# Three rows in flight for V, four for the experts, and a first tile started in another order

## The chip, the cores and the metric

The kernel runs on one core of a Trainium2 chip. The number that counts is the device time of one execution in microseconds, as the median over runs; less is better. The engines of the core are called by the profile's names: PE (TensorE), DVE (VectorE), ACT (ScalarE), POOL (GpSimd) and SP (SyncE, which only issues transfers here). PSUM is divided into eight banks, numbered 0 to 7.

## What is computed

A graph of N = 1250 nodes with 768 features runs through two graph attention layers and then through one transformer block. Cut to what matters:

```python
def _gat_layer(x, W, a_src, a_dst, b, src, dst, n):
    h = x @ W
    e = leaky_relu((h @ a_src)[src] + (h @ a_dst)[dst], 0.2)
    w = exp(e - segment_max(e, dst)[dst])
    alpha = w / segment_sum(w, dst)[dst]
    return segment_sum(h[src] * alpha[:, None], dst) + b

x = x + gat2(relu(gat1(layernorm(x))))          # 1250 x 768
x = x + ffn(layernorm(x))
def ffn(x):
    x = x + attention(layernorm(x) * g1 + b1)   # 12 heads of 64, x @ Wqkv, softmax, @ Wproj
    return x + moe(layernorm(x) * g2 + b2)      # 8 experts, top 2, 768 -> 384 -> 768, exact gelu
```

## The kernel before

Everything is float32 in quality: each product is made of three matmuls of rounded parts (`three`, lines 368 to 370: high by high, low by high, high by low). For each operand ACT copies the high part out of PSUM or SBUF ("hi", "higher"), and DVE or POOL subtracts it from the original to get the low part ("lo", "lower"). The 1250 nodes are ten tiles of 125 rows (T = 10). The order on each engine is written out by hand; semaphores are counted, and a wait such as `wait_ge(sem("tile_lo"), ...)` holds back everything behind it on its engine. Three stages matter here.

**The second graph layer.** For each tile t, ACT and DVE make a row block of attention weights in `lg2[:, t % 2]` (`sloped`, `leaky` L687, `exponential`, `weigh` L693). PE transposes it into banks 0 to 2 (`turned`, L591), ACT and DVE split the result into `pthi` and `ptlo` (`higher` L641, `lower` L698), and PE sums over the neighbours with 60 matmuls (`sums`, L368 to L370). `turned` of tile t+1 waits for `lower` of tile t, since both use banks 0 to 2. `agg_pe` gives PE's order: it turns tile t+1 ahead of the sums of tile t. `agg_act` and `agg_dve` give the others', with a step k for each tile. In steps 3 to 12 of this layer, `finish2` adds the sums to the residual, DVE takes mean and variance, ACT the root (`root`), DVE the reciprocal, and ACT writes two normalized rows (`rows2` L1847: `xab` and `xnb`). SP sends them to DRAM as `xa_d` and `xn_d` (`g2_rows`, L1356).

**The V stage.** V is the product of the normalized rows with a third of Wqkv. SP loads a tile of `xn_d` back into one of two buffers `vtin` (`v_in`, L1365). DVE applies scale and offset (`v_affine`, L565 and L567, 125x768 each). PE transposes into banks 0 and 1 (`v_turn`, L522, 6 instructions). ACT and DVE split (`v_higher` L543, `v_lower` L554). PE multiplies in two halves of 18 matmuls (`v_half`). The PE order is turn, half, turn, half: turn i+1 is followed by half i % 2 of tile i // 2, and the other halves come later, beside the first query-key work, which starts with `project`. `v_turn` of tile t waits for `v_lower` of tile t-1 (one pair of banks), and `v_in` of tile t for `v_turn` of tile t-2 (two buffers). `v_affine(3)` and later ones stand on DVE directly ahead of the `v_lower` of the tile before.

**The experts.** The (token, expert) pairs are sorted into TILES = 27 tiles of 128 slots. For tile j, POOL gathers 128 rows of 776 floats by an index (`gather`, L1557) into buffer j % 3. PE transposes them (`turn`, L1229), multiplies with W1 (`hidden`), transposes the gelu (`turn_h`, L1247) and multiplies with W2 (`output`). ACT and DVE split W1 and W2 anew for each tile (`split_w1`: L1892, L2382; `split_w2`: L1900, L2389, each 128x2304). ACT writes the weighted result (`row`, L1927), and POOL adds its rows to the output in DRAM by two indirect transfers, one for first and one for second choices (`add_first` L1563, `add_second` L1571). W2 comes through SP (L1437) into one of two buffers, issued when the `w2lo` of two tiles before is done. PE's order in the loop is hidden(i+1), turn(i+2), output(i), turn_h(i+1). POOL's is

```python
gather(0); gather(1); gather(2); gather(3)
pool.wait_ge(sem("route_dve"), ADDS)
for j in range(TILES):
    if j + 4 < TILES:
        gather(j + 4)
    add_first(j)
    add_second(j)
```

where `gather(j)` from j = 3 on waits until tile j-3 is transposed and its `weight` (L2408) is taken, and `add_first(j)` waits for `row(j)`.

## Time and profile before

| what | value |
|---|---|
| median of three runs | 1574.52 us (1572.43 to 1579.07) |
| the profiled execution: its own time, its span | 1568.86 us, 1567.1 us |
| PE, DVE, ACT, POOL busy | 91%, 74%, 62%, 32% of the span |
| mean granted TensorE clock | 0.964 of full speed |
| second layer from its first turn | about 419 to 543 us of the span |
| V stage (to the start of `project`) | about 543 to 592 us |
| experts | about 1334 to 1563 us |

Times below are microseconds from the start of the span, except durations in ns where the view says so. A row of the timeline is: start, duration, engine, line, operation, output tile <- input tiles, shapes, and in brackets how long the engine was idle before it and what it had waited for. PEclk is the granted clock as a share of full speed (2.4 GHz); 0.5 is 1.2 GHz. A matmul's duration overlaps the next one's, so starts are compared, not sums of durations.

### The profile page before, as it was taken

The page shows a single profiled execution, that of the slowest core. Times are in us where ns is not written, and L with a number is a line of the kernel's source. Part 1 is how long each engine was busy: PE and PEld are TensorE (multiplying, and loading weights), DVE is VectorE, ACT ScalarE, POOL GpSimd, SP SyncE. Part 2 cuts the span into 40 slices and gives each one's busy share as a digit, 9 for nine tenths or more (in the row PEclk, how much of TensorE's full clock was granted, in tenths as well). Part 3 has the DMA queues.
Part 4 walks back from the last instruction along what each step waited for, and adds up shares of the span by engine and source line. Part 5 has one row for each costly group of instructions (what it writes and reads, how often), then busy time and mean ns, then how long its engine had stood idle before and what let it go on. Part 6 is the DMA issues. An engine that isn't in the chain of part 4 may idle for free.

```text
span 1567.1 us, 25494 instructions
## 1 busy us (share of the span) xinstructions
PE 1424.7 (91%) x8979; PEld 1343.9 (86%) x8979; DVE 1154.7 (74%) x1752; ACT 968.8 (62%) x1656; POOL 508.2 (32%) x365
## 2 busy tenths in 40 slices
PE   3998799999699979999999999999988996799996
PEld 1896488999699979899898998989988996799995
DVE  6788889625779652486868868688687887788884
ACT  7996976522568322366857667576777311788884
POOL 2000000000000001244636446364466310488886
PEclk9999699999799999999999999999999997899998
DMA  7001000221225440000000000000001594699883
GB/s 196 2 1 41 1 10 21 82 85 53 100 64 162 137 149 1 1 21 1 21 0 0 20 0 20 0 0 0 20 22 41 163 282 94 213 251 249 244 231 102
DMA packets 59910, 121.49 MB, mean 78 GB/s; under 512 B 11152, under 2 KB 27156, under 8 KB 59824
## 3 DMA queue, kind: packets, MB, share of 16 engines
q1 hardware_dynamic: 48448, 98.09, 20.0%
q0 software_dynamic: 11376, 22.29, 6.6%
q8 instruction: 49, 0.80, 0.2%
q14 instruction: 37, 0.30, 0.1%
HBM read 89.57 MB, written 44.31 MB: 85 GB/s over the span
## 4 chain that ended last, share of the span: by engine, by line
PE 59%; DVE 10%; DMA 6%; issue 4%; ACT 2%; POOL 2%; ACTq 0%; SPq 0%; POOLq 0%; DVEq 0%
PE ps L368 11%; PE ps L369 11%; PE ps L370 11%; DMA xg<-xg_d,index 4%; PE ps L808 4%; PE ps L849 4%; PE ps L851 3%; PE ps L828 3%; PE ps L850 3%; PE ps L830 3%; DVE mcol L1050 2%; DMA vtin<-xn_d 2%; PE ps L591 1%; DVE prlo L1019 1%; PE ps L817 1%
## 5 line engine op out<-in xcount | busy, mean ns | idle before, releaser
L1019 POOL TENSOR_TENSOR prlo<-prob,prhi 125x500 fp32r<-125x500 f32 x180 | 249.0, 1389 | 273.0 <-ACT prob L961 272.3
L1050 DVE TENSOR_REDUCE mcol<-ps 125x1 f32<-125x1250 f32 x120 | 175.0, 1458 | 78.2 <-PE ps L808 77.6
L959 ACT ACTIVATE prhi<-ps 125x500 fp32r<-125x500 f32 x300 | 177.0, 590 | 74.9 <-PE ps L830 69.4
L849 PE MATMUL ps<-prhi,vhi 125*128 125x250 f32 x600 | 173.1, 288 | 10.4 <-POOL prlo L1019 4.8
L961 ACT ACTIVATE prob<-ps 125x500 f32<-125x500 f32 x300 | 176.4, 588 | 2.1 <-DVE prlo L1019 2.0
L1506 POOL MEMSET q<- 128x2500 f32 x1 | 2.2, 2187 | 532.4 <-PE ps L370 532.4
L851 PE MATMUL ps<-prlo,vhi 125*128 125x250 f32 x600 | 169.2, 282 | 0.0
L850 PE MATMUL ps<-prhi,vlo 125*64 125x250 f32 x600 | 168.2, 280 | 0.0
L1648 PE MATMUL ps<-ohs,ohd 128*125 128x417 bf16 x380 | 124.2, 389 | 39.2 <-DVE ohs L2063 38.6
L828 PE MATMUL ps<-qst,kst 128*125 128x250 f32 x600 | 156.6, 284 | 3.4 <-issue 1.4
L830 PE MATMUL ps<-q,k 128*125 128x250 f32 x600 | 153.7, 280 | 0.0
L368 PE MATMUL ps<-hhi,pthi 125*125 125x384 f32 x400 | 150.3, 376 | 0.0
L1019 DVE TENSOR_TENSOR prlo<-prob,prhi 125x500 fp32r<-125x500 f32 x120 | 106.9, 892 | 48.4 <-ACT prob L961 47.4
L369 PE MATMUL ps<-hhi,ptlo 125*125 125x384 f32 x400 | 136.2, 341 | 0.0
L370 PE MATMUL ps<-hlo,pthi 125*125 125x384 f32 x400 | 135.5, 339 | 0.0
L849 PEld LDWEIGHTS ps<-prhi,vhi 125*128 125x128 f32 x600 | 114.8, 191 | 16.9 <-DVE prlo L1019 6.6
L2063 DVE TENSOR_SCALAR ohs<-iota,scol,sval 128x420 bf16<-128x420 f16 x380 | 123.5, 384 | 0.0
L828 PEld LDWEIGHTS ps<-qst,kst 128*125 128x125 f32 x600 | 113.0, 188 | 10.6 <-issue 3.8
L1774 ACT ACTIVATE ohd<-iota,drel 128x125 bf16<-128x125 f16 x380 | 118.8, 389 | 0.3 <-POOLq L1473 0.3
L851 PEld LDWEIGHTS ps<-prlo,vhi 125*128 125x128 f32 x600 | 114.6, 191 | 0.0
L830 PEld LDWEIGHTS ps<-q,k 128*125 128x125 f32 x600 | 113.3, 189 | 0.0
L1648 PEld LDWEIGHTS ps<-ohs,ohd 128*125 128x125 bf16 x380 | 55.0, 146 | 66.8 <-DVE ohs L2063 46.7
(324 smaller groups left out, 4057.8 us busy)
## 6 DMA issues: line engine op xcount, KB each, us to landing
w2st<-in_L_ffn_W_dram SPq DMA_DIRECT2D x27, 1152.0 KB
w1all<-in_L_ffn_W_dram SPq DMA_DIRECT2D x8, 1152.0 KB, 9.3
wqst<-in_L_ffn_Wqkv_dram SPq DMA_DIRECT2D x12, 384.0 KB, 4.3
hid_d<-tin SPq DMA_DIRECT2D x10, 375.0 KB
hin<-hid_d SPq DMA_DIRECT2D x10, 375.0 KB
vtin<-xn_d SPq DMA_DIRECT2D x10, 375.0 KB
out_dram<-accr POOLq DMA_DIRECT2D x10, 375.0 KB, 9.0
xall<-in_x_dram SPq DMA_DIRECT2D x5, 672.0 KB
```

Source lines behind the costliest of these rows:

```text
L368: pe.matmul(o, lhi, rhi, start=start, stop=False)
L369: pe.matmul(o, llo, rhi, start=False, stop=False)
L370: return pe.matmul(o, lhi, rlo, start=False, stop=stop)
L828: pe.matmul(o, kst[:, e, kt * P:(kt + 1) * P], qst[:, e, g * GQ:(g + 1) * GQ], start=True, stop=False)
L830: last = pe.matmul(o, k2[:, e, kt * P:(kt + 1) * P], q2[:, e, g * GQ:(g + 1) * GQ], start=False, stop=True)
L849: pe.matmul(ps[:, b:b + GQ], vhi[:, e, kt, :], hi, start=kt == 0, stop=False)
L850: pe.matmul(ps[0:HD, b:b + GQ], vlo[:, e, kt, :], hi, start=False, stop=False)
L851: last = pe.matmul(ps[:, b:b + GQ], vhi[:, e, kt, :], lo, start=False, stop=kt == T - 1)
L959: act.activation(prhi[:, n % RING, :], bank(3 + n % 3, P, 2 * GQ), ACT.Exp, scale=float(HD) ** -0.5)
L1019: eng.tensor_tensor(prlo[:, n % RING, :], prob[:, n % 3, :], prhi[:, n % RING, :].bitcast(f32), ALU.subtract)\
L1050: dve.tensor_reduce(mcol[:, e, t:t + 1], ps[0:P, 0:N], AX.X, ALU.max, negate=True).then_inc(sem("max"), 1)
L1648: pe.matmul(into, hots(b)[:, i, :], ohs[:, g % OHS, 0:PACK], start=u == 0, stop=u == WINDOW - 1).then_inc(sem("oh_free"), 1)
```

## The change

Three parts.

1. V stage. `vtin` has three buffers. `v_turn` uses banks 0 and 1 for even tiles and 2 and 3 for odd ones, and so waits for `v_lower` of tile t-2. `v_in(0)`, `v_in(1)` and `v_in(2)` are issued on SP after `g2_rows(3)`, `(4)` and `(5)`, `v_in(3)` after `g2_rows(8)`, and `v_in(4)` now after `g2_rows(9)`. From tile 3 on, `v_in` waits for `v_turn` of tile t-3. On DVE the affine steps of tiles 0 to 2 move to steps 7 to 9 of the second layer, and later ones stand two tiles ahead and behind `v_lower`. On ACT `v_higher(2)` moves ahead of the root of tile 9.
2. Second layer, tile 0. PE makes the first half of tile 0's sums ahead of the turn of tile 1; ACT makes `higher(0)` ahead of `exponential(1)`, DVE `weigh(0)` ahead of `leaky(1)` and `lower(0)` ahead of `weigh(1)`.
3. Experts. A fourth buffer `xg3` (in the place of a tile that is dead by then); `gather(j)` waits for tile j-4, and one more gather stands ahead of the first add.

```diff
-    vtin = put("vtin", [P, 2, D], f32, at=put.end)
+    vtin = put("vtin", [P, 3, D], f32, at=put.end)
...
+    xg3 = put("xg3", [S, ROW], f32, at=put.end - 4 * D)
...
         def rows(j):
-            return xg2[:, :] if j % 3 == 2 else xg[:, j % 3, :]
+            return (xg[:, 0, :], xg[:, 1, :], xg2[:, :], xg3[:, :])[j % 4]
...
         def v_turn(pe, t):
-            u = t % 2
-            if t == 0:
+            if t < 2:
                 pe.wait_ge(sem("agg_lo"), 2 * T + 1)
             else:
-                pe.wait_ge(sem("tile_lo"), 2 * T + t + 2)
+                pe.wait_ge(sem("tile_lo"), 2 * T + t + 1)
             pe.wait_ge(sem("v_row"), t + 1)
             for k in range(KD):
-                at = k // 3 * BANK + k % 3 * P
-                last = pe.transpose(ps[:, at:at + P], vtin[:, u, k * 128:(k + 1) * 128], ident[0:P, 0:P])
+                at = (t % 2 * 2 + k // 3) * BANK + k % 3 * P
+                last = pe.transpose(ps[:, at:at + P], vtin[:, t % 3, k * 128:(k + 1) * 128], ident[0:P, 0:P])
...
             turned(pe, n, 0, 0)
+            sums(0, 0, range(T))
+            turned(pe, n, 1, 1)
+            sums(0, 0, range(T, 2 * T))
             with pe.Fori(0, T // 2 - 1) as i:
-                turned(pe, n, 2 * i + 1, 1)
-                sums(2 * i, 0)
                 turned(pe, n, 2 * i + 2, 0)
                 sums(2 * i + 1, 1)
-            turned(pe, n, T - 1, 1)
-            sums(T - 2, 0)
+                turned(pe, n, 2 * i + 3, 1)
+                sums(2 * i + 2, 0)
             v_turn(pe, 0)
             sums(T - 1, 1)
...
             maximum(1)
+            weigh(dve, n, 0)
             leaky(dve, n, 1)
-            weigh(dve, n, 0)
             maximum(2)
...
             for t in range(T - 2):
                 g2_rows(t)
-                if t == 3:
-                    v_in(0)
-                    v_in(1)
-            v_in(2)
+                if 3 <= t < 6:
+                    v_in(t - 3)
             g2_rows(T - 2)
             v_in(3)
+            g2_rows(T - 1)
             v_in(4)
-            g2_rows(T - 1)
             v_in(5)
...
             def gather(j):
-                if j >= 3:
-                    pool.wait_ge(sem("rows_raw"), T + j - 2)
-                    pool.wait_ge(sem("gslot"), j - 2)
+                if j >= 4:
+                    pool.wait_ge(sem("rows_raw"), T + j - 3)
+                    pool.wait_ge(sem("gslot"), j - 3)
...
             pool.wait_ge(sem("route_dve"), ADDS)
+            gather(4)
             for j in range(TILES):
-                if j + 4 < TILES:
-                    gather(j + 4)
+                if j + 5 < TILES:
+                    gather(j + 5)
                 add_first(j)
                 add_second(j)
...
                 if k == T + 1:
                     v_higher(act, 1)
+                    v_higher(act, 2)
...
-                if k in (T - 2, T - 1):
-                    v_affine(dve, k - (T - 2))
-                if k == T:
-                    v_lower(dve, 0)
-                    v_affine(dve, 2)
-                if k == T + 1:
-                    v_lower(dve, 1)
+                if T - 3 <= k < T:
+                    v_affine(dve, k - (T - 3))
+                if k in (T, T + 1):
+                    v_lower(dve, k - T)
             agg_dve(dve, order, 1, before2, finish2, after2)
+            v_affine(dve, 3)
             for t in range(2, T):
-                if t + 1 < T:
-                    v_affine(dve, t + 1)
                 v_lower(dve, t)
+                if t + 2 < T:
+                    v_affine(dve, t + 2)
```

DVE at the start of the second layer, before (L673 to L682 are the maximum of a tile, L687 `leaky`, L693 `weigh`):

```order
L687 SCALAR_TENSOR_TENSOR lg2_66<-esb_65,ed_55,lg2_66 125x1250 [waits agg_sl]
L693 SCALAR_TENSOR_TENSOR lg2_66,wsum_58<-lg2_66,cnt_63 125x1250 [waits agg_e]
L673 ISA cand_67,zsum_57<-esb_65,far_64 125x1250 [waits far_ready]
```

And the same place of the changed kernel (L695 is `weigh`, L689 `leaky`):

```order
L695 SCALAR_TENSOR_TENSOR lg2_66,wsum_58<-lg2_66,cnt_63 125x1250 [waits agg_e]
L689 SCALAR_TENSOR_TENSOR lg2_66<-esb_65,ed_55,lg2_66 125x1250 [waits agg_sl]
L675 ISA cand_67,zsum_57<-esb_65,far_64 125x1250 [waits far_ready]
```

The weights of tile 0 are now finished one 125x1250 pass earlier.

SP's queue at the end of the second layer, before, from the load of row tile 2 to that of tile 5 (`vtin` is the tile's buffer; the rows between are the outputs of tiles 8 and 9):

```order
L1365 DMA vtin<-xn_d 125x768 [waits xn_out,tile_raw]
L1356 DMA out_dram<-xres 112x768 [waits x1_row]
L1356 DMA out_dram<-xres 13x768
L1356 DMA xa_d<-xab 112x768 [waits xa_row]
L1356 DMA xa_d<-xab 13x768
L1356 DMA xn_d<-xnb 112x768 [waits xn_row]
L1356 DMA xn_d<-xnb 13x768
L1365 DMA vtin<-xn_d 125x768 [waits xn_out,tile_raw] x2
```

And of the changed kernel, from the outputs of tile 9 on (L1361 is the line of the outputs, L1370 that of the loads):

```order
L1370 DMA vtin<-xn_d 125x768 [waits xn_out,tile_raw]
L1361 DMA out_dram<-xres 112x768 [waits x1_row]
L1361 DMA out_dram<-xres 13x768
L1361 DMA xa_d<-xab 112x768 [waits xa_row]
L1361 DMA xa_d<-xab 13x768
L1361 DMA xn_d<-xnb 112x768 [waits xn_row]
L1361 DMA xn_d<-xnb 13x768
L1370 DMA vtin<-xn_d 125x768 [waits xn_out,tile_raw] x2
```

In the first of these the pair of loads is that of tiles 3 and 4, behind the outputs of tile 8. In the second it is that of tiles 4 and 5, behind the outputs of tile 9; tile 3's is the row at the top. The load of tile 2 is gone from here to a place three output groups earlier.

POOL at the start of the experts, before:

```order
L1557 DMA xg_145<-xg_d,index_176 128x776 [waits gates_out,route_dve,sum_out1,sum_out0]
L1557 DMA xg_145<-xg_d,index_176 128x776
L1557 DMA xg2_194<-xg_d,index_176 128x776
L1557 DMA xg_145<-xg_d,index_176 128x776 [waits gslot,rows_raw]
L1557 DMA xg_145<-xg_d,index_176 128x776 [waits gslot,rows_raw,route_dve]
L1563 DMA out_0_dram<-yrow_146,index_176 1250x768 [waits y_row2]
```

And of the changed kernel:

```order
L1560 DMA xg2_195<-xg_d,index_176 128x776
L1560 DMA xg3_181<-xg_d,index_176 128x776
L1560 DMA xg_145<-xg_d,index_176 128x776 [waits gslot,rows_raw,route_dve]
L1560 DMA xg_145<-xg_d,index_176 128x776 [waits gslot,rows_raw]
L1566 DMA out_0_dram<-yrow_146,index_176 1250x768 [waits y_row2]
```

The fourth gather waits for nothing more, and a sixth stands ahead of the first add.

## Rows read from the trace of the kernel before

**Rows 1.** The page: the chain that ended last, shares of the span by line.

```profile
PE ps L368 11%; PE ps L369 11%; PE ps L370 11%; DMA xg<-xg_d,index 4%; PE ps L808 4%; PE ps L849 4%; PE ps L851 3%; PE ps L828 3%; PE ps L850 3%; PE ps L830 3%; DVE mcol L1050 2%; DMA vtin<-xn_d 2%; PE ps L591 1%; DVE prlo L1019 1%; PE ps L817 1%
```

**Rows 2.** Busy time by stretch: length, five engines, PEclk, DMA share, GB/s.

```profile
407.00:427.00 20.00, 7.33 (x30) 5.89 (x29) 18.35 (x30) 13.54 (x15) 0.00 (x0) 0.65 0.56 196
451.00:520.00 69.00, 69.00 (x415) 69.00 (x415) 59.81 (x113) 53.65 (x59) 0.00 (x0) 1.00 0.45 143
543.00:592.00 49.00, 38.30 (x216) 36.23 (x215) 27.48 (x36) 15.36 (x19) 10.30 (x5) 0.93 0.41 126
1352.00:1381.00 29.00, 29.00 (x181) 28.55 (x179) 25.75 (x25) 25.73 (x24) 18.21 (x8) 1.00 0.84 235
1381.00:1540.00 159.00, 149.98 (x901) 144.47 (x901) 131.27 (x120) 131.09 (x120) 136.95 (x61) 0.99 0.88 243
```

**Rows 3.** Waits from 1352 to 1541 us: us in total, times, longest.

```profile
PEld ps L1229 <- DMA xg<-xg_d,index: 13.9, 16, 2.3
```

**Rows 4.** Timeline of PE, experts: the turns of tiles 3, 4, 25 and 26.

```profile
1359.19 0.82 PE L1229 MATMUL ps<-ident,xg 128*128 128x128 f32 x6
...
1366.46 0.82 PE L1229 MATMUL ps<-ident,xg 128*128 128x128 f32 x6
...
1531.19 0.87 PE L1229 MATMUL ps<-ident,xg 128*128 128x128 f32 x6 [1.94 <-DMA xg<-xg_d,index]
...
1540.05 0.81 PE L1229 MATMUL ps<-ident,xg 128*128 128x128 f32 x6
```

**Rows 5.** Timeline of POOL: gathers of tiles 3, 6 and 26, first add.

```profile
1341.85 0.95 POOL L1557 DMA_INDIRECT xg<-xg_d,index  x1 [4.54 <-DVE gjunk L2408]
...
1360.65 2.58 POOL L1563 DMA_INDIRECT out_dram<-yrow,index  x1 [8.67 <-ACT yrow L1927]
...
1374.53 2.61 POOL L1557 DMA_INDIRECT xg<-xg_d,index  x1 [0.30 <-PE ps L1229]
...
1529.86 2.63 POOL L1557 DMA_INDIRECT xg<-xg_d,index  x1 [0.30 <-ACT yrow L1927]
```

**Rows 6.** Timeline of DVE, experts: a low part of W2, one of W1.

```profile
1370.24 2.56 DVE L2389 TENSOR_TENSOR w2lo<-w2st,w2hi 128x2304 fp32r<-128x2304 f32 x1 [0.28 <-ACT w2hi L1900]
...
1373.69 2.56 DVE L2382 TENSOR_TENSOR w1lo<-w1all,w1hi 128x2304 fp32r<-128x2304 f32 x1 [0.43 <-ACT w1hi L1892]
```

**Rows 7.** Timeline of ACT, experts: the high part of W2, two tiles on.

```profile
1383.10 2.14 ACT L1900 ACTIVATE w2hi<-w2st 128x2304 fp32r<-128x2304 f32 x1
```

**Rows 8.** The page: transfer issues, KB each, median us from issue to landing.

```profile
w1all<-in_L_ffn_W_dram SPq DMA_DIRECT2D x8, 1152.0 KB, 9.3
```

**Rows 9.** The chain in order of time, V stage: start, us, what.

```profile
534.60 6.79 DMA vtin<-xn_d
...
541.41 0.97 DVE vtin L565
...
545.37 1.03 ACT xab L1847
...
548.22 7.52 DMA vtin<-xn_d
```

**Rows 10.** Timeline of PE, V stage: turns of tiles 4 and 9, `project`.

```profile
564.10 0.80 PE L522 MATMUL ps<-ident,vtin 125*128 125x125 f32 x6
...
588.41 0.86 PE L522 MATMUL ps<-ident,vtin 125*128 125x125 f32 x6 [1.94 <-DVE xtlo L554]
...
592.26 0.35 PE L368 MATMUL ps<-xthi,wqhi 128*128 128x418 f32 x1
```

**Rows 11.** Timeline of PE, second layer: turns 0, 1, first sum, turn 2.

```profile
418.88 2.46 PE L591 MATMUL ps<-ident,lg 125*125 125x125 f32 x10 [9.33 <-DVE lg L693]
...
424.35 2.43 PE L591 MATMUL ps<-ident,lg 125*125 125x125 f32 x10 [3.01 <-DVE ptlo L699]
...
426.44 0.66 PE L368 MATMUL ps<-hhi,pthi 125*125 125x384 f32 x1
...
438.64 1.25 PE L591 MATMUL ps<-ident,lg 125*125 125x125 f32 x10
```

More of the change, by code:

```diff
@@ L543, in v_higher @@
             act.activation(xthi[:, :, t * P:(t + 1) * P].rearrange("p (a k) c -> p a k c", a=2),
-                           two(0, 128, 3 * P).rearrange("p a (k c) -> p a k c", k=3), ACT.Copy).then_inc(sem("tile_hi"), 1)
+                           two(t % 2 * 2, 128, 3 * P).rearrange("p a (k c) -> p a k c", k=3), ACT.Copy).then_inc(sem("tile_hi"), 1)
         def v_out(act, t):
@@ L606, in agg_pe, with sums @@
         def agg_pe(pe, n):
-            def sums(t, u):
-                for i in range(2 * T):
+            def sums(t, u, steps=range(2 * T)):
+                for i in steps:
                     triple_sum(pe, n, t, u, i)
             turned(pe, n, 0, 0)
+            sums(0, 0, range(T))
+            turned(pe, n, 1, 1)
+            sums(0, 0, range(T, 2 * T))
             with pe.Fori(0, T // 2 - 1) as i:
-                turned(pe, n, 2 * i + 1, 1)
-                sums(2 * i, 0)
                 turned(pe, n, 2 * i + 2, 0)
                 sums(2 * i + 1, 1)
-            turned(pe, n, T - 1, 1)
-            sums(T - 2, 0)
+                turned(pe, n, 2 * i + 3, 1)
+                sums(2 * i + 2, 0)
             v_turn(pe, 0)
@@ L658, in agg_act @@
             for k in range(T + 3):
+                if k == 0:
+                    higher(act, n, 0)
                 if k + 1 < T:
@@ L715, in step @@
             def step(k):
+                if k == 0:
+                    lower(dve, n, 0)
                 if k + 1 < T:
                     weigh(dve, n, k + 1)
-                if k < T:
+                if 0 < k < T:
                     lower(dve, n, k)
@@ L995, in attention_act @@
             for t in range(T // 2 - 1):
-                v_higher(act, 2 * t + 2)
+                if t:
+                    v_higher(act, 2 * t + 2)
                 v_higher(act, 2 * t + 3)
```

20 lines of the change are left out of this document (10 added, 10 removed).

## The prediction

> **What bounds the kernel now.** I read the chain that ended last first. Most of the lines that it names are products on PE, but two entries are transfers that PE ends up waiting for: the gather of the experts' rows, 4% of the span, and the load of V's rows, 2% [rows 1]. Those are the two transfers that the change gives more buffers. I then read the busy time by stretch [rows 2]. PE is busy without a gap in the second layer from 451 to 520 us, and also at the start of the experts (29.00 of 29.00 us). It is not busy in three places: from 407 to 427 us, where the second layer starts (7.33 of 20 us, at a granted clock of 0.65); from 543 to 592 us, the V stage (38.30 of 49 us, clock 0.93); and in the experts from 1381 to 1540 us (149.98 of 159 us). The change touches exactly those three, and PE's order of work is otherwise the same, so the sum is made of what each gives back.
>
> **Experts: a fourth buffer.** No computation is added or removed. There are 27 gathers and 54 adds as before; only the order on POOL moves by one gather. At its best PE takes one tile in 1366.46 - 1359.19 = 7.27 us, from the turn of tile 3 to that of tile 4 [rows 4]. From the turn of tile 4 to that of tile 26 it needs 173.6 us for 22 tiles, 7.89 us each. At 7.27 it would be 159.9 us, so 13.7 us are lost. The list of waits puts them down to one cause: the weight load of the transpose waits for the gather 16 times, 13.9 us in all [rows 3].
>
> Why does the gather come late? The first one that waits for nothing takes POOL 0.95 us; that of tile 6 takes 2.61 us and begins while DVE is inside `w1lo` [rows 5]. DVE's pass ends at 1376.25, and the gather ends 0.89 us after it, at 1377.14 [rows 6]. So the gather has to wait for the end of the pass and then takes its usual time. POOL goes at DVE's pace, not at its own. After the descriptors are out, the rows need 4 to 6 us more (tile 25 and others), and the turn is due some 4.3 us later: there is no slack. The gather of tile j in the changed kernel stands where that of tile j-1 stood, a full tile earlier, and so gains about 7.3 us of slack against lateness of at most 2.3 us [rows 3]. What it has to wait for, the turn and the weight of tile j-4, is done long before. The extra gather falls into the 8.67 us in which POOL waits for the first result [rows 5], so it costs nothing. If that cover were gone it would cost 3 us once. Queued behind each gather are the two adds of its round, and they are served as before.
>
> Upper bound: all 13.7 us. Lower bound: POOL keeps the pace that it shows from tile 6 to tile 26, 155.3 us for 20 gathers, 7.77 us each [rows 5]; then the last gather still comes one place earlier, and PE's end, which hangs on it, moves up by 7.7 us. I take 12, near the upper one: at 7.27 us a tile the transfer share of 0.88 becomes 0.88 x 7.89 / 7.27 = 0.95, and a few waits should remain.
>
> The Trainium skill has a rule on this, "SBUF — State Buffer", section "Who interferes with whom": a DVE instruction with two SBUF inputs and a GpSimd instruction that reads SBUF shut each other out for a whole instruction. By that rule, the trace agrees: 2.61 us against 0.95 us. The rule speaks against the change in one way: if the lockout makes POOL the slowest engine, more buffers move the gathers only once, and the experts give 7.7 us and not 12.
>
> **V stage.** Nothing is computed more or less here either. Before, the chain runs: DVE stands still until the load of tile 2, issued at 534.60, has landed after 6.79 us; the affine passes follow at 541.41; only then come DVE's statistics for tile 8, ACT's normalized rows at 545.37, SP's outputs and, behind them, the next load at 548.22, which takes 7.52 us [rows 9]. With the change tile 2 is loaded three output groups earlier, so its affine steps are done in the second layer, where DVE is busy 59.8 of 69 us and PE covers it [rows 2]. Then PE goes on from 543 us with turn 1, a half, turn 2 and another half without waiting: turn plus half is 592.26 - 588.41 = 3.85 us [rows 10]. Turn 3 starts at about 551.
>
> The next thing to be late is the load of tile 4. It now stands on SP behind the outputs of tile 9, and those stand behind ACT's `v_higher(2)`. My reckoning, in the clock of the trace before: turn 2 done 547.5, `v_higher(2)` 0.8, the root and DVE's reciprocal 0.7, two rows of ACT 1.9 (1.03 each at most [rows 9]), SP's outputs 0.9: issue at 551.8. The load takes 6.8 to 7.5 us [rows 9], and two affine passes of 0.97 us follow [rows 9]: turn 4 at 560.7 to 561.3, say 561.0. Before it is at 564.10 [rows 10], so 3.1 us are won up to here. PE waits some 5.5 us for it and runs at half clock after that. What half clock costs I take from the second layer: PE's first sums take 438.64 - 426.44 = 12.2 us [rows 11], where at full clock 70 instructions take 70 x 69 / 415 = 11.6 us [rows 2], less 1.1 for the turn, 10.5: an extra 1.7 us. From turn 4 to `project` there are six turns and halves, 6 x 3.85 = 23.1 us, plus 1.7: 24.8 us, and `project` starts at 585.8. Later loads are issued when the turn of three tiles before is done, 11.5 us ahead of need against 6 to 7.5 us of load, and hide. Before, `project` starts at 592.26. V gives 6.5 us. Bounds: if the loads of tiles 6 to 9 stay chained, only 3; if the load of tile 4 took no wait at all, 592.26 less (543 + 9 x 3.85) = 14.6. I stay with 6.5, since SP's order leaves the load of tile 4 where it is.
>
> **Second layer, tile 0.** DVE's `weigh(0)` is one pass of 1.4 us earlier, so turn 0 starts at 417.5 and ends at 419.9. The split takes the 3.0 us that it takes now (421.34 to 424.35) [rows 11]. The sums start at 422.9 and not at 426.44. They and turn 1 take 10.5 + 1.1 us at full clock, and half clock adds 1.7 us, or 2.7 us if it lasts as long after the restart as it does now. Turn 2 then starts at 436.2 to 437.2 and not at 438.64: 1.4 to 2.4 us, I take 1.9. Nothing is behind it: turn 2 needs `weigh(2)` and `lower(1)`, done some 2 us ahead. If these were late, it would be 0. From turn 2 on PE is the bound until 543 us, so the gain is carried through.
>
> **Sum.** 12.0 + 6.5 + 1.9 = 20.4 us. The profiled execution took 1568.86 us, its span being 1567.1, and would become 1548.5. The median of the three runs is 1574.52, 5.7 above it; taken from that, 1554.1 us.
>
> **Rivals.** Half a per cent is 7.9 us, about what can be told from no change here.
>
> *POOL's pace.* The lock makes POOL itself the slowest engine in the experts. For it: POOL's gaps are 0.30 us throughout [rows 5]. Against it: PE went at 7.27 us with the same adds and gathers beside it, and POOL's alone need 5 us. Experts 7.7: 1574.5 - 16.1 = 1558.4.
>
> *Transfers fill up, no gain in the experts.* W2's load is issued when `w2lo` of tile 3 ends, at 1372.80 [rows 6], and is needed by `w2hi` of tile 5 at 1383.10 [rows 7]: 10.3 us. Loads of the same size needed 9.3 us in the stage before [rows 8]. A faster pace loads the transfer engines more (share 0.95), and once the load takes over 10.3 us ACT waits. At 11.5 us a tile lasts 7.89 us again and the experts give nothing: 1574.5 - 8.4 = 1566.1. Against it: ACT never waits for W2 now, at a share of 0.84 and a pace of 7.27 us [rows 2].
>
> *The same, to a loss.* The other two parts give 8.4 us, so the experts would have to lose 16.3 us for the whole to be 7.9 us slower: 0.7 us in each of 24 tiles, 8.6 us a tile. W2's load has two tiles less 4.2 us, so it decides from 13.0 us on, 3.7 us over the row. At 8.7 us a tile the time is about 1585.
>
> *V stays chained.* ACT's and DVE's new places make tile 9's outputs later still, and with them the loads: V gives 3 and not 6.5, 1557.6. I count it with the forecast.
>
> **How the numbers follow.** Forecast, with V chained or not: 0.70. POOL's pace: 0.14. Transfers without a gain: 0.10. The loss: 0.03. Another effect of any sign: 0.03. All of the first two are faster than by 0.5%, and half of the third: 0.88 with a little of the last. Within 0.5%: 0.08; slower: 0.04. Range: the lower end is 13.7 + 2.4 + 9 = 25 us off and 3 us for the spread of medians, 1546. The upper end takes in POOL's pace, with a V stage at its lower bound and 3 us of spread, and reaches toward the third case: 1564.
>
> **What the profile would show.** Right: turns of tiles 5 to 26 every 7.3 to 7.4 us with hardly any wait for the gather, and gathers of 2.6 us as before; the second layer's turn 2 some 12 us after the first sums; turn 4 of V after a wait of about 5 us, for the load, and none after that. Wrong: ACT's `w2hi` waiting for its load; POOL's gathers 7.7 us apart and PE waiting for them; a `project` later than 43 us after the second layer's last sum; turn 2 of the second layer waiting for `weigh(2)`.

## The result and the profile after

The changed kernel takes 1558.61 us, the median of 4 runs (1551.40 to 1560.81); the kernel before took 1573.47 beside it (4 runs). The ratio is 0.9893, with a 95% interval of 0.985 to 0.9936: 14.9 us by the medians, 16.8 by the ratio, where 20.4 were forecast. A second measurement of the same code on another occasion gave 1552.15 us, ratio 0.9897 (0.9867 to 0.9927). The predicted 1554 lies between the two medians, but the second was taken where the kernel before ran at 1569.70 us, 3.8 us less than beside the first. What was saved is 15 to 17 us both times, and 20.4 were forecast.

The profiled execution took 1560.81 us, the slowest of its four. Read stage by stage, it shows less in the experts than the forecast. The windows of the changed kernel (length, PE, PEld, DVE, ACT, POOL busy, PEclk, DMA share, GB/s), against [rows 2]:

```profile
541.00:587.00 46.00, 37.29 (x222) 36.20 (x222) 26.80 (x31) 13.42 (x17) 10.13 (x5) 0.93 0.38 119
1345.00:1425.00 80.00, 80.00 (x498) 79.26 (x497) 71.96 (x67) 70.00 (x65) 63.73 (x27) 1.00 0.85 240
1425.00:1530.00 105.00, 98.36 (x596) 94.36 (x594) 87.31 (x81) 88.04 (x80) 92.81 (x41) 1.00 0.85 239
```

For 80 us PE has no gap in the experts, which the kernel before managed for 29. After that it is idle again, 6.6 us in 105. The last of the three rows also points at the reason: POOL is busy 92.81 us, and its 41 instructions each stand behind a gap of 0.30 us, 12.3 us in all. Together that is 105.1, the whole window: POOL never waits for work there. Its busy time holds the time in which DVE's passes hold it up, so it is not all work of its own.

The waits from 1345 to 1532 us (us in total, times, longest), against [rows 3]:

```profile
PEld ps L1234 <- DMA xg<-xg_d,index: 10.6, 11, 1.8
...
ACT w2hi L1905 <- DMA w2st<-in_L_ffn_W_dram: 1.4, 3, 0.8
```

PE's turns in the experts, tiles 4, 12, 14 and 26, against [rows 4]:

```profile
1361.30 0.82 PE L1234 MATMUL ps<-ident,xg 128*128 128x128 f32 x6
...
1419.32 0.82 PE L1234 MATMUL ps<-ident,xg 128*128 128x128 f32 x6
...
1435.02 0.88 PE L1234 MATMUL ps<-ident,xg 128*128 128x128 f32 x6 [0.74 <-DMA xg<-xg_d,index]
...
1530.49 0.88 PE L1234 MATMUL ps<-ident,xg 128*128 128x128 f32 x6 [1.12 <-DMA xg<-xg_d,index]
```

From tile 4 to tile 12 a tile takes (1419.32 - 1361.30) / 8 = 7.25 us, as forecast. From tile 12 to tile 26 it takes 111.17 / 14 = 7.94. Over all 22 tiles 169.2 us stand against 173.6 before: 4.4 us, not 12 to 13.7, and less than the 7.7 that the forecast gives as its lower bound. What happened between is on POOL (L1560 the gather, L1566 and L1574 the two adds), gathers 9 to 13:

```profile
1383.89 2.60 POOL L1560 DMA_INDIRECT xg<-xg_d,index  x1 [0.30 <-PE ps L1234]
...
1395.91 3.01 POOL L1574 DMA_INDIRECT out_dram<-yrow,index  x1 [0.30 <-issue]
1399.22 2.09 POOL L1560 DMA_INDIRECT xg<-xg_d,index  x1 [0.30 <-issue]
1401.62 3.72 POOL L1566 DMA_INDIRECT out_dram<-yrow,index  x1 [0.30 <-DVE gjunk L2411]
1405.64 3.15 POOL L1574 DMA_INDIRECT out_dram<-yrow,index  x1 [0.30 <-ACT yrow L1932]
1409.10 3.37 POOL L1560 DMA_INDIRECT xg<-xg_d,index  x1 [0.30 <-issue]
...
1420.10 2.72 POOL L1560 DMA_INDIRECT xg<-xg_d,index  x1 [0.30 <-issue]
```

These four rounds take 36.21 us, 9.05 each. At 7.25 they would take 29.0, so POOL loses 7.2 us, one tile, while PE loses nothing yet: its next turns still come 7.24 to 7.26 us apart, on gathers that POOL had made ahead (its lead). From tile 13 on that lead is gone. The same stretch on ACT and DVE:

```profile
1392.77 2.13 ACT L1905 ACTIVATE w2hi<-w2st 128x2304 fp32r<-128x2304 f32 x1 [0.76 <-DMA w2st<-in_L_ffn_W_dram]
```

```profile
1394.94 2.56 DVE L2392 TENSOR_TENSOR w2lo<-w2st,w2hi 128x2304 fp32r<-128x2304 f32 x1 [1.14 <-ACT w2hi L1905]
...
1397.88 2.55 DVE L2385 TENSOR_TENSOR w1lo<-w1all,w1hi 128x2304 fp32r<-128x2304 f32 x1
...
1401.33 2.56 DVE L2392 TENSOR_TENSOR w2lo<-w2st,w2hi 128x2304 fp32r<-128x2304 f32 x1
```

W2's load was 0.76 us late for ACT. DVE's `w2lo` came later, `w1lo` then followed it closely, and the next `w2lo` began at 1401.33, 6.39 us after the late one, at once behind DVE's other work. POOL's first add began at 1401.62, the usual 0.30 us after the gather's end at 1401.31, and met `w2lo` 0.29 us into its pass. (The profile names `gjunk`, DVE's weight pass, as its releaser, but `add_first` waits in the code for ACT's row alone, and that was ready at 1398.18.) It ended at 1405.34, 1.45 us after the pass, and took 3.72 us instead of 1.57.

The V stage, PE's turns 1, 4 and 7 and `project`, against [rows 10]:

```profile
541.72 0.80 PE L522 MATMUL ps<-ident,vtin 125*128 125x125 f32 x6
...
560.69 1.49 PE L522 MATMUL ps<-ident,vtin 125*128 125x125 f32 x6 [7.01 <-DVE vtin L566]
...
575.50 0.83 PE L522 MATMUL ps<-ident,vtin 125*128 125x125 f32 x6 [1.49 <-DVE vtin L566]
...
586.95 0.35 PE L369 MATMUL ps<-xthi,wqhi 128*128 128x418 f32 x1
```

and the chain in order of time (start, us, what), against [rows 9]:

```profile
550.57 8.00 DMA vtin<-xn_d
...
...
562.21 8.19 DMA vtin<-xn_d
570.42 3.95 DVE vtin L564
```

From turn 1 to `project` it takes 586.95 - 541.72 = 45.23 us. Before, turn 1 began at 542.90 and `project` at 592.26, 49.36 us. V has given 4.1 us.

The second layer's first turns (turns 0 and 2 on L590, and one instruction of the stage ahead on L490), against [rows 11]:

```profile
410.09 0.48 PE L490 MATMUL ps<-diag,ones 125*125 125x125 f32 x2 [0.33 <-DVE diag L474]
418.47 2.46 PE L590 MATMUL ps<-ident,lg 125*125 125x125 f32 x10 [7.90 <-DVE lg L695]
...
437.46 1.25 PE L590 MATMUL ps<-ident,lg 125*125 125x125 f32 x10
```

From the stage ahead to turn 2 it is 27.37 us. Before, that instruction stood at 409.06 and turn 2 at 438.64, 29.58 us: 2.2 us won.

### The profile page after: what moved, and what is told of

Read it like the earlier page. It is cut to its first block, busy times and chain, and to the rows that moved or that the text cites. A ratio compares the mean times of both kernels' runs of the same rounds, so it can differ in the third digit from the quotient of the medians.

```text
span 1558.9 us, 25492 instructions
## 1 busy us (share of the span) xinstructions
PE 1420.0 (91%) x8979; PEld 1342.8 (86%) x8979; DVE 1160.3 (74%) x1752; ACT 969.1 (62%) x1656; POOL 513.1 (33%) x365
## 4 chain that ended last, share of the span: by engine, by line
PE 62%; DVE 9%; DMA 5%; issue 3%; ACT 2%; POOL 2%; POOLq 0%; DVEq 0%; ACTq 0%; SPq 0%
PE ps L369 12%; PE ps L370 12%; PE ps L371 12%; PE ps L812 4%; PE ps L853 4%; PE ps L855 3%; PE ps L832 3%; PE ps L854 3%; PE ps L834 3%; DMA xg<-xg_d,index 3%; DVE mcol L1055 2%; PE ps L590 1%; DMA vtin<-xn_d 1%; DVE prlo L1024 1%; PE ps L821 1%
## 5 line engine op out<-in xcount | busy, mean ns | idle before, releaser
L1024 DVE TENSOR_TENSOR prlo<-prob,prhi 125x500 fp32r<-125x500 f32 x120 | 112.1, 935 | 46.7 <-ACT prob L965 45.7
L853 PEld LDWEIGHTS ps<-prhi,vhi 125*128 125x128 f32 x600 | 115.2, 192 | 16.8 <-DVE prlo L1024 7.1
L832 PEld LDWEIGHTS ps<-qst,kst 128*125 128x125 f32 x600 | 112.8, 188 | 10.5 <-issue 3.8
```

The costliest lines, as they stand in the source:

```text
L832: pe.matmul(o, kst[:, e, kt * P:(kt + 1) * P], qst[:, e, g * GQ:(g + 1) * GQ], start=True, stop=False)
L853: pe.matmul(ps[:, b:b + GQ], vhi[:, e, kt, :], hi, start=kt == 0, stop=False)
L1024: eng.tensor_tensor(prlo[:, n % RING, :], prob[:, n % 3, :], prhi[:, n % RING, :].bitcast(f32), ALU.subtract)\
```

## The experiments

Below, POOL is "in step" as long as its gathers follow each other at PE's pace, 7.25 us a tile, and "out of step" where they take longer. Two theories of what limits the experts are tested: (1) POOL's instructions beside DVE's long passes, once POOL has fallen out of step; (2) the transfers. Every kernel here was timed against the kernel before on its own chip, whose median there was 1569.7 to 1571.4 us; only ratios and traces are compared across chips.

**p_experts, p_v, p_first: one part of the change each; p_all: all of it again.** The edits are the three parts of the diff, here with a line or two of each.

```diff
 p_experts
-            return xg2[:, :] if j % 3 == 2 else xg[:, j % 3, :]
+            return (xg[:, 0, :], xg[:, 1, :], xg2[:, :], xg3[:, :])[j % 4]
 p_v
-    vtin = put("vtin", [P, 2, D], f32, at=put.end)
+    vtin = put("vtin", [P, 3, D], f32, at=put.end)
 p_first
             leaky(dve, n, 0)
             maximum(1)
+            weigh(dve, n, 0)
             leaky(dve, n, 1)
-            weigh(dve, n, 0)
```

> The kernel before with the four buffers of gathered rows in the experts alone. The recorded prediction gives this part 12.0 us (7.7 to 13.7). The trace of the changed kernel shows less: from turn 4 to turn 26 of the experts 169.2 us where the kernel before took 173.6, so 4.4 us, plus about 1.7 us for the missing wait of turn 3 to 4. Theory 1 (after tile 9 POOL needs more than 7.26 us for a tile, since its gathers and adds find no gap between VectorE's passes with two operands in SBUF): turns 4 to 12 are 7.26 us apart, then the gaps grow to about 8 us, because POOL loses a tile of lead; time 5 to 8 us below the kernel before. Theory 2 (the transfers are the limit): the same time, but then the gathers of POOL wait for nothing of VectorE and TensorE waits for gathers that were issued in time. The slip seen in the changed kernel's trace may also be a matter of the moment at which this loop starts; then turns stay 7.26 us apart to the end here and the time is 11 to 13 us below the kernel before.

> The kernel before with the V stage's two pairs of banks and three row buffers alone. The recorded prediction gives this part 6.5 us (3 to 14.6). The trace of the changed kernel shows 49.4 us from the second turn to the projection before and 45.2 us after: 4.1 us, with one wait of 7.0 us at turn 4 for the load of tile 4 and one of 1.5 us at turn 7. If the parts add, the time is 4 to 5 us below the kernel before; the end of the V stage at about 587 to 588 us instead of 592.3.

> The kernel before with the second layer's first tile in the other order alone. The recorded prediction gives this part 1.9 us (1.4 to 2.4); the trace of the changed kernel shows 2.2 us against the end of the stage ahead. Expected 2 us below the kernel before; a loss would say that what was gained there is lost in the work behind it.

> The changed kernel again, on the same chip as the three parts, to see whether they add up. The recorded prediction gives 20.4 us, the first measurement gave 14.9 us. If the loss against the prediction is POOL's lost tile of lead in the experts (theory 1), then executions without that loss would be faster by up to 7 or 8 us than those with it, and the times of this kernel spread more than those of the kernel before. If the transfers are the limit (theory 2), the times lie close together at 13 to 16 us below the kernel before.

Measured, all on one chip:

| kernel | median us | lowest to highest | ratio, 95% interval | from the ratio | forecast |
|---|---|---|---|---|---|
| before | 1569.70 (23 runs) | 1566.42 to 1574.83 | | | |
| p_experts | 1558.74 (6) | 1555.29 to 1560.83 | 0.9924, 0.9908 to 0.9941 | 11.9 us | 12.0 |
| p_v | 1564.26 (12) | 1560.82 to 1571.10 | 0.9973, 0.9958 to 0.9987 | 4.2 us | 6.5 |
| p_first | 1568.73 (12) | 1561.57 to 1571.95 | 0.9991, 0.9977 to 1.0005 | 1.4 us | 1.9 |
| p_all | 1552.15 (6) | 1549.11 to 1564.98 | 0.9897, 0.9867 to 0.9927 | 16.2 us | 20.4 |

The parts add up within the intervals: 11.9 + 4.2 + 1.4 = 17.5 us against 16.2 together. `p_first` alone can't be told from no change. The experts' part, which my reading of the first trace had put at 5 to 8 us, gives all of the forecast's 12 (9.3 to 14.4 by the interval). The trace of `p_all` says why the first trace misled. In the experts, PE's turns of tiles 4 and 26:

```profile
1365.49 0.82 PE L1234 MATMUL ps<-ident,xg 128*128 128x128 f32 x6
...
1525.04 0.82 PE L1234 MATMUL ps<-ident,xg 128*128 128x128 f32 x6
```

159.55 us for 22 tiles, 7.25 each, with no wait for a gather after the first tile's. One round of POOL there, gather, two adds and the next gather, and DVE's `w2lo` in it:

```profile
1395.31 2.62 POOL L1560 DMA_INDIRECT xg<-xg_d,index  x1 [0.30 <-ACT yrow L1932]
1398.23 1.57 POOL L1566 DMA_INDIRECT out_dram<-yrow,index  x1 [0.30 <-DVE gjunk L2411]
1400.11 2.16 POOL L1574 DMA_INDIRECT out_dram<-yrow,index  x1 [0.30 <-issue]
1402.57 2.60 POOL L1560 DMA_INDIRECT xg<-xg_d,index  x1 [0.30 <-ACT yrow L1932]
```

```profile
1398.28 2.56 DVE L2392 TENSOR_TENSOR w2lo<-w2st,w2hi 128x2304 fp32r<-128x2304 f32 x1 [0.29 <-ACT w2hi L1905]
```

In step, POOL takes 2.62 + 1.57 + 2.16 + 3 x 0.30 = 7.25 us a tile, and PE takes 7.25. Part of the gather's 2.62 and of the second add's 2.16 is waiting for the end of a pass, so a small slip is made good: in this trace two rounds of 7.74 and 7.93 us, behind loads of W2 that were 0.40 and 0.58 us late, were followed by rounds of 6.74 and 6.84. A whole tile is never made good, since POOL gets one round in for each of DVE's.

The rows also show on how little the step hangs. The first add begins 0.05 us ahead of `w2lo`, and both take their usual time, 1.57 and 2.56 us. In all 21 rounds of this trace from gather 6 on it begins ahead of `w2lo`, in 18 of them by 0.02 to 0.05 us, and never takes more than 1.58. In the profile of `p_experts` POOL is in step up to gather 20 (1467.72 us) and then takes 29.10 us for three rounds (to 1496.82), 9.7 each, again right behind a `w2hi` that had waited 0.75 us for its load. There too the next `w2lo` came early (6.36 us after the late one), and the first add began 0.33 us after it:

```profile
1478.27 3.68 POOL L1564 DMA_INDIRECT out_dram<-yrow,index  x1 [0.30 <-DVE gjunk L2410]
```

```profile
1477.94 2.56 DVE L2391 TENSOR_TENSOR w2lo<-w2st,w2hi 128x2304 fp32r<-128x2304 f32 x1
```

From turn 4 to turn 26 that execution took 162.9 us. The same code can thus lose its lead early, late or never.

`p_all` lost 4.6 us elsewhere, at the very start (ACT):

```profile
1340.45 2.12 ACT L1905 ACTIVATE w2hi<-w2st 128x2304 fp32r<-128x2304 f32 x1 [4.25 <-DMA w2st<-in_L_ffn_W_dram]
```

The first tile's `gel` is queued behind `w2hi`, and that waits for the first load of W2: 4.25 us here, 0.32 in the first trace, nothing in the kernel before's. PE's turns 1 and 2 are 10.54 us apart here and 5.94 in the first trace. This is a second source of spread. Whether the change has a part in it isn't settled: in the profiles without the fourth buffer (the kernel before, `p_v`, `p_first`) that wait was 0, 0.20 and 0.30 us, in those with it 0 to 4.25.

**w2_third: from the third tile on, W2's load with a third of its bytes.** The rest of the buffer keeps old values, so the kernel leaves out a part of the computation; no instruction of the engines is missing.

```diff
-                sp.dma_start(w2st[:, j % 2, :, :], w2.rearrange("e (k r) f -> e r k f", r=128)[ds(e, 1), :, :, :]
+                q = KF if j < 2 else 1
+                sp.dma_start(w2st[:, j % 2, 0:q, :], w2.rearrange("e (k r) f -> e r k f", r=128)[ds(e, 1), :, 0:q, :]
```

> The changed kernel, but from the third tile of the experts on W2's load brings one third of its bytes (the other two thirds of the buffer keep old values, so this part of the computation is left out); every instruction of the engines stays. The traces so far: in one execution of the changed kernel POOL stays in step with TensorE to the end (27 gathers, 7.25 us apart, no gather waited for), in another it falls out of step at tile 10, and in the experts-only kernel at tile 23; each time ScalarE's w2hi had waited 0.75 us for W2's load just before. Theory 1 (a late W2 load only starts the slip, the price is POOL's own instructions beside VectorE's passes): here w2hi waits for no load, POOL's gathers stay 7.25 us apart, the time is 1549 to 1553 us on a chip where the kernel before takes 1570, and the six times lie within some 4 us of each other. Theory 2 (the transfers themselves are the limit, gathers land late for lack of room): gathers land in 5 us or less instead of 7.4 and the time falls by more than 2 us below the best executions of the changed kernel, which have no slip. Theory 3 (the slip has nothing to do with W2's load): some executions still take 1557 to 1565 us.

Measured: 1550.81 us, 4 runs within 1550.70 to 1552.43; ratio 0.9877 (0.9859 to 0.9896). The window from 1425 us on:

```profile
1425.00:1525.00 100.00, 100.00 (x622) 99.10 (x621) 90.22 (x82) 90.35 (x84) 86.49 (x41) 1.00 0.70 153
```

The transfer share falls to 0.70, gathers land after 5.7 us in the median instead of the 7.8 of the first trace, and PE is no faster than in `p_all`. So the transfers do not set the pace when all is in step; PE does, and theory 2 in its direct form falls. The four times lie close together where those of the changed kernel spread over 16 us (ten executions, 1549.1 to 1565.0). That fits the view that late W2 loads start the loss, but four executions are few: about half of the changed kernel's ten were below 1553 too.

**short_passes: DVE's long passes cut.**

```diff
-                dve.tensor_tensor(w2lo[:, u, :, :].rearrange("p k c -> p (k c)"), w2st[:, u, :, :].rearrange("p k c -> p (k c)"),
-                                  w2hi[:, u, :, :].rearrange("p k c -> p (k c)").bitcast(f32), ALU.subtract).then_inc(sem("w2_lo"), 1)
+                for c in range(KF):
+                    last = dve.tensor_tensor(w2lo[:, u, c, :], w2st[:, u, c, :], w2hi[:, u, c, :].bitcast(f32), ALU.subtract)
+                last.then_inc(sem("w2_lo"), 1)
```

and `w1lo` in two passes in the same way.

> The changed kernel with VectorE's two long passes cut: w1lo in two of 1152 columns, w2lo in three of 768; the same sums. In the traces an instruction of POOL that begins while such a pass of 2.56 us runs ends 0.9 to 1.5 us after the pass has ended (3.3 to 3.8 us instead of 1.57 for the first add). Theory 1 (POOL's wait for the end of VectorE's pass is the price of a slip): with passes of 0.9 and 1.3 us an instruction of POOL waits at most that long, the adds never take over 3 us, POOL's tile stays under 7.26 us in any order, and no execution slips: 1549 to 1554 us beside 1570 of the kernel before, or some us more if VectorE's added starts (3 a tile, of some 0.06 us) count. Theory 2 (transfers): the late loads are as before, and the times spread as the changed kernel's do, 1549 to 1565.

Measured: 1554.78 us, 1548.62 to 1560.57; ratio 0.9892 (0.9864 to 0.9919). As theory 1 says, POOL gets room. Its windows, and the waits from 1345 to 1525 us:

```profile
1425.00:1525.00 100.00, 97.20 (x601) 95.58 (x600) 88.79 (x119) 86.76 (x82) 68.26 (x39) 1.00 0.93 252
```

```profile
ACT w2hi L1905 <- DMA w2st<-in_L_ffn_W_dram: 6.1, 5, 2.1
...
PEld ps L369 <- DVE htlo L2407: 3.5, 3, 1.4
```

POOL is busy 68.26 of 100 us, and no gather is waited for any more. But the times still spread over 12 us, so theory 1's forecast of them is wrong. In this execution, which took 1559.76 us, `w2hi` waits for W2's load and PE for what stands behind it. From turn 4 to turn 26 it took 163.5 us, 3.9 more than `p_all`, and the first tile's `w2hi` had waited 3.52 us. Here a late load costs directly, with POOL out of the way.

**w2_chunks: short passes, and W2's load in three pieces as its buffer comes free.**

```diff
-                if j >= 2:
-                    sp.wait_ge(sem("w2_lo"), j - 1)
+                for c in range(KF):
+                    if j >= 2:
+                        sp.wait_ge(sem("w2_lo"), KF * (j - 2) + c + 1)
+                    sp.dma_start(w2st[:, j % 2, c:c + 1, :], ...)
```

> The short-passes kernel with W2's load cut in three as well: each third of the buffer is loaded as soon as VectorE's pass over that third of the tile two before has ended, instead of all of it after the last; all bytes are loaded. So far: with a third of W2's bytes the times lay at 1550.7 to 1552.4, while short passes alone gave 1548.6 to 1560.6, and in its slow profile ScalarE's w2hi waited six times (7.3 us) for W2's load. Theory 1 (what starts a slip is that the load of W2 is late against its window of some 10 us): the first two thirds start some 1.7 and 0.9 us earlier, w2hi waits for the load hardly ever, and all six times lie at 1548 to 1552 us. Theory 2 (the transfer engines are full, so that an earlier issue only lands as late): w2hi waits as before, the times spread over 8 us or more again. Three issues for one may cost transfer time of their own: then the median is above that of short passes (1554.8).

Measured: 1553.01 us, 1548.12 to 1559.07; ratio 0.9898 (0.9879 to 0.9918). In its profile (1548.12 us) `w2hi` waits for no load after the first tile, and PE is busy for all 90 us from 1420 to 1510. The spread is 11 us all the same, and not the 4 that theory 1 gave. The profile shows only one of the fast executions, so what slowed those at 1557 and 1559 isn't known.

**two_late: W2's load issued later, in two tiles.**

```diff
                 if j >= 2:
                     sp.wait_ge(sem("w2_lo"), j - 1)
+                if j in (8, 9):
+                    sp.wait_ge(sem("rows_hi"), T + j + 1)
```

> The changed kernel with W2's load of two tiles alone, 8 and 9 of 27, issued some 2.6 us later than now: SP waits for ScalarE's xhi of the same tile as well. No byte and no instruction of the engines is added. In step with TensorE a load has 9.76 us from its buffer's release to its w2hi (1379.07 to 1388.83 in the trace of the repeated changed kernel), so with 2.6 us less a load of 7.1 us (the one median seen) is just late and one of 9.9 us by 2.7 us. Theory 1 (a late W2 load puts VectorE's pass where POOL's first add begins, and POOL loses its lead for good): POOL's gathers stay 7.25 us apart up to about the 11th and fall to 9 to 11 us apart in the two or three after it; TensorE then waits for gathers to the end or for several tiles, and the time lies at 1556 to 1565 us in nearly every execution. Theory 2 (a late load costs its own lateness and nothing more): one or two waits of at most 2.7 us at w2hi, POOL back at 7.25 us at once, and the times spread as the changed kernel's do (1549 to 1565, five of ten below 1553).

Measured: 1554.44 us, 1547.25 to 1560.03; ratio 0.9897 (0.9871 to 0.9924), the spread of the changed kernel. The profile (1547.25 us) contradicts theory 1. ACT, then POOL's gathers 11 to 14, then PE's turns:

```profile
1397.88 2.13 ACT L1907 ACTIVATE w2hi<-w2st 128x2304 fp32r<-128x2304 f32 x1 [2.23 <-DMA w2st<-in_L_ffn_W_dram]
```

```profile
1394.74 2.63 POOL L1562 DMA_INDIRECT xg<-xg_d,index  x1 [0.30 <-ACT yrow L1934]
...
1401.40 2.09 POOL L1562 DMA_INDIRECT xg<-xg_d,index  x1 [0.30 <-issue]
...
1410.69 2.56 POOL L1562 DMA_INDIRECT xg<-xg_d,index  x1 [0.30 <-PE ps L1234]
...
1417.86 2.64 POOL L1562 DMA_INDIRECT xg<-xg_d,index  x1 [0.30 <-ACT yrow L1934]
```

```profile
1401.21 0.82 PE L1234 MATMUL ps<-ident,xg 128*128 128x128 f32 x6
1409.82 0.82 PE L1234 MATMUL ps<-ident,xg 128*128 128x128 f32 x6
```

The load was 2.23 us late, three times as late as in the two executions that fell out of step. POOL took 15.95 us for two rounds instead of 14.5, and was back in step at once. PE had lost the same: 8.61 us for one tile instead of 7.25. So POOL's lead over PE was as large as before, and the late load cost about 1.4 us and nothing after. Theory 2 described this run rightly. A late load does not by itself end the step. In the two traces with a loss PE lost nothing at the time, and POOL alone fell behind. The next `w2lo` came 6.36 us after the late one here too, but POOL had run on while DVE waited: its first add began 2.44 us ahead of that `w2lo`, inside `w1lo`, and took 3.02 us. What differs between the three traces is where the add met the passes.

**v_order and v_order_more: SP's loads for the V stage placed earlier.**

```diff
 v_order
-            g2_rows(T - 1)
-            v_in(4)
-            v_in(5)
+            g2_rows(T - 1, lambda n: v_in({"x1": 4, "xa": 5}[n]) if n != "xn" else None)
 v_order_more, on top of it
+            v_in(6)
+            v_in(7)
             for n in ("x1", "xa", "xn"):
                 sp.wait_ge(sem(f"{n}_out"), 32 * T)
             load_qk(0)
-            for t in range(6, T):
+            for t in range(8, T):
                 v_in(t)
```

`v_order` also moves ACT's `v_higher(2)` behind the rows of tile 9.

> The changed kernel with the load of V's tile 4 ahead of the output of tile 9's x1 on SP, that of tile 5 ahead of the output of its xa, and ScalarE's copy of V's tile 2 after the rows of tile 9. In the changed kernel's trace the load of tile 4 was issued at 550.57, 8.8 us after the turn (541.72) that frees its buffer, behind two outputs of tile 9; it took 8.0 us, and TensorE waited 7.01 us at turn 4. Issued at about 543.5 it is there by 551.5, so VectorE has the row ready by 553.5 and turn 4 waits for next to nothing (turn 3 and its six products end at about 553.7). Theory 1 (the place on SP is what made tile 4 late): turn 4 at 554 to 555 instead of 560.69, the end of the stage 5 to 7 us earlier, the time 4 to 7 us below the changed kernel. Theory 2 (the load is slow because other transfers run beside it, or the next load becomes the bound): turn 4 still waits over 3 us or turn 5 or 6 waits in its place, and the time moves by less than 2 us.

> V's order with the loads of V's tiles 6 and 7 ahead of the wait for the landing of tile 9's outputs and of the first q and k weights. V's order alone moved the wait from turn 4 (7.01 us) to turn 6 (6.58 us): the load of tile 6 was issued at 556.19, 5.6 us of that behind the outputs' landing, though its buffer was free at 550.7. The end of the stage, counted from the second turn, came only 2.4 us earlier (42.8 us instead of 45.2). Theory 1 (SP's order sets it): issued at 550.7 the load of tile 6 is there at 558.5, the wait at turn 6 falls to about 1 us, and the projection starts 37 to 38 us after the second turn; the best executions at 1543 to 1546 us. Theory 2 (each removed wait comes back at the next load): a wait of over 4 us at turn 8 or 9, or at the projection for the q and k weights, and a gain under 2 us.

Measured: `v_order` 1554.73 us, 1549.42 to 1565.44, ratio 0.9913 (0.9883 to 0.9944); `v_order_more` 1547.45 us, 1543.22 to 1555.44, ratio 0.986 (0.9835 to 0.9885). PE in the V stage of `v_order`, turns 1, 4, 6 and `project`, and SP's queue:

```profile
542.32 0.80 PE L522 MATMUL ps<-ident,vtin 125*128 125x125 f32 x6
...
553.71 0.80 PE L522 MATMUL ps<-ident,vtin 125*128 125x125 f32 x6
...
568.05 1.49 PE L522 MATMUL ps<-ident,vtin 125*128 125x125 f32 x6 [6.58 <-DVE vtin L566]
...
585.12 0.35 PE L369 MATMUL ps<-xthi,wqhi 128*128 128x418 f32 x1
```

```profile
555.10 0.99 SPq L1376 DMA_DIRECT2D wqst<-in_L_ffn_Wqkv_dram  x2
556.19 13.63 SPq L1371 DMA_DIRECT2D vtin<-xn_d  x4
```

The wait at turn 4 is gone, and turn 6 waits 6.58 us instead: SP sat until 555.10 for the landing of tile 9's outputs before it issued the load of tile 6. Theory 2 of this pair is the one that held. The saving of 2.4 us (45.23 to 42.80 from turn 1 to `project`) is lost in the spread of the times, and the 4 to 7 us that I expected are not there. With two more loads ahead, turns 8 and `project`:

```profile
571.63 1.49 PE L522 MATMUL ps<-ident,vtin 125*128 125x125 f32 x6 [3.38 <-DVE vtin L566]
...
582.01 0.35 PE L369 MATMUL ps<-xthi,wqhi 128*128 128x418 f32 x1
```

582.01 less 541.43, where its turn 1 began, is 40.58 us: 4.65 less than in the changed kernel, not the 7 to 8 that I expected. The wait has moved once more, to turn 8, and halved. This is the fastest kernel of the study: its fastest execution is 5.9 us below the changed kernel's fastest of ten (1549.11), though the intervals of the two ratios overlap.

**both_orders and best: the combinations.** `both_orders` is short passes with `v_order`; `best` has short passes, W2 in pieces and `v_order_more`. They have no edits of their own.

> The edits of short passes and of V's order together, since they touch different stages. If each does what the first theory says of it, the gains add: 1543 to 1549 us beside 1570 of the kernel before. If the short passes cost VectorE time that the path feels, this one is slower than V's order alone in its best executions.

> The short passes, W2's load in thirds and V's order with four loads ahead, all together. If both first theories hold, the gains add: all times at 1542 to 1547 us beside 1570 of the kernel before, with a spread of at most 4 us.

Measured: `both_orders` 1551.96 us (1549.69 to 1556.55, 5 runs), ratio 0.9885 (0.9866 to 0.9905); `best` 1550.10 us (1546.10 to 1552.05, 4 runs), ratio 0.9859 (0.9839 to 0.988). The edits to W2 add nothing that can be measured to the V order, and both missed their forecasts, 1543 to 1549 and 1542 to 1547. The profiled execution of `best` had the other loss: `w2hi` of the first tile waited 3.73 us for its load. Its four times lie within 6 us, those of `p_experts` without these edits too, so nothing can be built on that.

## Why the prediction was right, point by point

**Experts, 12.0 us: right.** The part alone gave 11.9 us, and the mechanism is the forecast's: with a gather made a tile earlier, PE's waits for gathers go. At the upper bound, 13.7, PE was to go at 7.27 us; in `p_all` it took 159.55 us for the 22 tiles, 14.0 less than before. At the lower one, 7.7, POOL keeps its own pace; in the first trace it does so from tile 13 on. That bound was too high for a single execution, because it let POOL keep the 7.77 us a tile of the kernel before: the first trace takes 160.6 us from gather 6 to gather 26, 8.03 each, and wins 4.4 us. The choice of 12 was in part luck. It stood for a few waits at a higher transfer share, and those did not come. I put what lies between 14.0 and 11.9 down to executions that fall out of step or wait for the first load of W2; no run separates the two. The rival "POOL's pace" was therefore not false, only a part of the truth: it is what an execution falls into. What I gave as its counter-argument, that POOL's instructions alone need 5 us, was beside the point, since they never run alone. In step they take 7.25. The rule of the Trainium skill, "SBUF — State Buffer", section "Who interferes with whom", that the two engines shut each other out for a whole instruction, agrees with the first trace where DVE begins first: the add that began 0.29 us into DVE's pass took 3.72 us and not 1.57. Where POOL begins first, these traces show no such thing in the experts: behind an add that began 0.05 us ahead, `w2lo` took its 2.56 us as ever.

**"As before, a few waits should remain": not seen.** In step there were none at all; out of step, in the first trace, there were eleven. The transfer share did rise to 0.96 in one window of `p_all`, as worked out (0.95), without slowing PE.

**V stage, 6.5 us: the mechanism right, the size off by 2.3.** The load of tile 2 no longer holds PE up: it was issued at 515.63 us and not at 534.60, two output groups earlier (not three, as the text ahead and the forecast say; this changes no term). The place of the next wait was right. The load of tile 4 was issued 8.85 us after turn 1, where the forecast has 551.8 - 542.9 = 8.9. Two terms were too small. The load took 8.00 us and not 6.8 to 7.5, so that turn 4 began 18.97 us after turn 1 and not 18.1; the wait was 7.01 us and not 5.5. And "later loads hide" failed: from turn 4 to `project` it took 26.26 us and not 24.8, 1.49 of it a wait at turn 7. There the load of tile 7 took 8.19 us, and DVE's affine pass 3.95 us instead of 0.96, because POOL's `wqlo` had begun 0.37 us before it:

```profile
570.05 3.50 POOL L1482 TENSOR_TENSOR wqlo<-wqst,wqhi 128x1536 fp32r<-128x1536 f32 x1 [25.92 <-ACT wqhi L917]
```

`wqlo` ends at 573.55 and DVE's pass at 574.37, 0.82 us later. Here DVE is the one shut out. I had read that lockout in the experts and did not look for it in this stage.

**Second layer, 1.9 us: right.** 2.2 us by the trace; by the clock 1.4 (-0.8 to 3.6), which no change would fit as well. Turn 2 began 13.53 us after the first sums (at 423.93), as the forecast's terms have it (10.5 + 1.1 + 1.7 to 2.7); its list of signs says 12 and does not fit them.

**The sum.** 17.5 us as the parts' sum and 16.2 measured together, against 20.4. What is missing is V's 2.3 us and, in some executions, POOL's lost tile (in the first trace the 22 tiles took 169.2 us and not 159.6) or a late first load of W2 (4.6 us in `p_all`). The forecast's chances for "faster by over 0.5%" add up to 0.89 by its own terms, not 0.88.

**What stays open.** Why one execution falls out of step and another does not. Two traces show the first slip, an add that begins 0.3 us behind the start of `w2lo` instead of just ahead; no experiment moved that add alone, so how far it may slip is not measured. Both losses followed a `w2hi` that was 0.75 us late, a load that was 2.23 us late did not bring one about, and kernels in which POOL has a fifth of its time free (68.26 us busy and 39 gaps of 0.30 in 100) spread as widely. A third of W2's bytes gave four even times. That may point to the transfers as the origin, but it is not shown.

## What to carry to other kernels

When an engine's busy time and its fixed gaps add up to the time of a loop's round, as POOL's 7.25 us do here, a further buffer pays in full only until the engine loses a whole round; look at a second execution before you trust one trace's pace, and at how far an instruction stands from the pass that would hold it up. A load that is moved forward uncovers the next one in the same queue: three edits here moved one wait from turn 2 to turn 4, to turn 6 and to turn 8, and each was worth only the difference. So list what stands ahead of each load on its queue, waits for landings included, before you size the gain. Measure the parts of a change on one chip: here that corrected what one profile had told wrongly.

## What the runs showed of the hardware that I had not expected

The time of POOL's indirect transfer instructions depends on where they meet DVE's passes with two operands in SBUF. One that begins clear of a pass, if only 0.02 us ahead of it, takes 0.95 us (gather) or 1.57 (add). One that begins inside a pass ends 0.82 to 0.90 us after the end of the pass (gather) or 1.41 to 1.53 (add; first trace and `p_all`), so that an add 0.29 us into a pass of 2.56 us takes 3.72. With the passes cut to a third and a half, POOL's busy share fell from 0.88 to 0.68 for the same number of transfers. The transfer engines took a share of 0.90 to 0.94 (`p_all`, `w2_chunks`) while PE was busy without a gap. And the changed kernel spread over 16 us (1549.11 to 1564.98, 6 runs) where the kernel before spread over 8.4 (1566.42 to 1574.83, 23 runs). `p_v` and `p_first` spread over 10 us in 12 runs each, `p_experts` over 5.5 in 6, so no one part can be named as the cause.
